# Storing x1 straight into the result, with the expert tiles scatter-adding there

## What is computed

```python
x = x + gnn(layernorm(x))            # relational graph convolution over 21,250 edges, 8 relations,
                                     # then tanh(u) * z + xn * (1 - z), z = [u, xn] @ w_gate + b_gate
# experts, on n = layernorm(x):
scores = softmax(n @ gate_w.T)       # 8 experts
top_scores, sel = top_k(scores, 2)   # each token goes to its 2 best
# tokens sorted by expert; for each expert e:
y = (silu(t @ w1[e]) * (t @ w3[e])) @ w2[e]       # 1024 -> 256 -> 1024
out = zeros.at[token].add(y * score)
x = x + out
```

## Time and profile before

| | |
|---|---|
| median of 3 runs | 1827.71 us |
| the profiled execution's own time | 1829.91 us |
| its span, first to last instruction | 1828.2 us |
| mean granted TensorE clock | 0.973 of full speed |
| PE busy / PEld busy | 1707.0 us (93%) / 1399.1 us (77%) |
| DVE / ACT / POOL busy | 1095.8 (60%) / 726.4 (40%) / 756.2 us (41%) |
| HBM traffic | 241.19 MB read, 102.15 MB written, 188 GB/s |

### The profile page before, as it was taken

How to read it: one execution, slowest core, us unless ns; L and a number is a source line. 1 busy time by engine, 2 the same in 40 slices (tenths; PEclk the granted TensorE clock), 3 DMA queues, 4 the chain that set the end, 5 groups by cost and what they waited for, 6 DMA issues and landing times. The chain is left out here.

```text
span 1828.2 us, 22117 instructions
## 1 busy us (share of the span) xinstructions
PE 1707.0 (93%) x7873; PEld 1399.1 (77%) x7873; DVE 1095.8 (60%) x1444; ACT 726.4 (40%) x1230; POOL 756.2 (41%) x663
## 2 busy tenths in 40 slices
PE   7999999999999999999998999989789958999993
PEld 6888888888888888888776777767678846878882
DVE  8555656665464342424599898899789876333200
ACT  2316656631231312121365565555522103454551
POOL 1001222226775656302355554545265515455531
PEclk9999999999999999999999999999899968999997
DMA  5236555466224343434788888888744436877645
GB/s 204 93 117 229 167 177 181 156 195 198 93 87 161 110 150 122 143 130 146 296 262 293 256 289 267 266 286 265 261 176 167 153 117 219 231 183 211 135 89 151
DMA packets 141050, 339.69 MB, mean 186 GB/s; under 512 B 19332, under 2 KB 35764, under 8 KB 140864
## 3 DMA queue, kind: packets, MB, share of 16 engines
q0 software_dynamic: 50816, 159.29, 29.2%
q1 hardware_dynamic: 90128, 179.00, 29.0%
HBM read 241.19 MB, written 102.15 MB: 188 GB/s over the span
## 5 line engine op out<-in xcount | busy, mean ns | idle before, releaser
L1056 POOL DMA_INDIRECT gathered<-Y,edge_row x184 | 220.5, 1198 | 218.2 <-PE banks L1215 189.4
L625 ACT ACTIVATE ghi<-gathered,edge_w 128x1024 fp32r<-128x1024 f32 x184 | 211.5, 1151 | 170.8 <-DMA gathered<-Y,edge_row 156.9
L945 DVE SCALAR_TENSOR_TENSOR glo<-gathered,edge_w,ghi 128x1024 fp32r<-128x1024 f32 x184 | 232.6, 1281 | 52.8 <-ACT ghi L625 51.1
L1032 POOL DMA_INDIRECT edge_w<-INV,edge_key x184 | 208.4, 1133 | 116.5 <-DMA edge_w<-INV,edge_key 84.9
L1073 PE MATMUL banks<-whi,xhi 128*128 128x512 f32 x640 | 252.7, 395 | 0.6 <-DVE xlo L768 0.6
L1075 PE MATMUL banks<-whi,xlo 128*128 128x512 f32 x640 | 249.8, 390 | 0.0
L1074 PE MATMUL banks<-wlo,xhi 128*128 128x512 f32 x640 | 249.7, 390 | 0.0
L1214 PE MATMUL banks<-ghi,sel 128*128 128x512 f32 x368 | 149.0, 405 | 25.6 <-DVE glo L945 24.3
L575 ACT ACTIVATE ring_hi<-raw_chunk 128x512 fp32r<-128x512 f32 x112 | 66.5, 624 | 207.5 <-PE banks L1177 127.6
L1215 PE MATMUL banks<-glo,sel 128*128 128x512 f32 x368 | 144.4, 392 | 0.0
L1073 PEld LDWEIGHTS banks<-whi,xhi 128*128 128x128 f32 x640 | 120.7, 189 | 25.5 <-DVE xlo L768 1.2
(11 more groups left out here) (316 smaller groups left out, 3670.9 us busy)
## 6 DMA issues: line engine op xcount, KB each, us to landing
raw<-in_L_ffn_w SPq DMA_DIRECT2D x24, 1024.0 KB
Y<-y_out SPq DMA_DIRECT2D x80, 256.0 KB
t_set<-in_L_gnn_weight POOLq DMA_DIRECT2D x64, 256.0 KB
TW<-t_set POOLq DMA_DIRECT2D x64, 256.0 KB
raw_chunk<-TW SPq DMA_DIRECT2D x64, 256.0 KB
w_stage<-in_L_gnn_weight SPq DMA_DIRECT2D x30, 512.0 KB, 5.0
raw_chunk<-in_L_gnn_weight SPq DMA_DIRECT2D x48, 256.0 KB
Y<-half_v SPq DMA_DIRECT2D x40, 256.0 KB
```

The source lines that it names most:

```text
L625: nc.scalar.activation(ghi[:, t % HR], gath[t % GR][:], ACT.Copy, scale=edge_w[:, t:t + 1]).then_inc(g_hi, 1)
L945: v.scalar_tensor_tensor(glo[t % GR][:], gath[t % GR][:], edge_w[:, t:t + 1], ghi[:, t % HR].bitcast(F32), ALU.mult, ALU.subtract).then_in ...
L1032: nc.gpsimd.indirect_dma_start(out=edge_w[:, t:t + 1], out_offset=None, in_=INV, in_offset=bass.IndirectOffsetOnAxis(ap=edge_key[:, t:t + ...
L1056: nc.gpsimd.indirect_dma_start(out=gath[t % GR][:], out_offset=None, in_=Y, in_offset=bass.IndirectOffsetOnAxis(ap=edge_row[:, t:t + 1], a ...
```

## The change

X1 is gone. In the gate stage x1 is stored straight into the result, of the last tile only its 98 rows, and the store for the dummy rows is gone. The scatter-adds go to the result, and the five copies at the end are gone with their wait. So the padded lanes need other rows, since the result has no dummy ones. A padded lane p of expert e now adds its zeros to row p, unless the token p is itself in the last tile of expert e; then it takes a row of 0 to 127 whose token is not there (some_row). No lane of a tile then adds zeros to a row to which another lane of the same tile adds its output. For this VectorE computes last_at (the position at which the last tile of each expert begins), in_last and spare (for the first 128 tokens) before it waits for the token lists. Then TensorE transposes spare (one small transpose), VectorE takes a maximum over it and spreads it, TensorE brings it to all lanes (one product with 8 rows), and VectorE picks for each tile its expert's entry (pad_row, 128x28x8) and puts it into add_i. The semaphore rt_poh now also counts these two hand-overs, and rt_placed (formerly rt_tok) the two answers. They lie in PSUM bank 6, in columns beside the logits; so TensorE waits for score_ready before its first output product into that bank (`outputs`).

```diff
--- before.py
+++ after.py
@@ -118,8 +118,6 @@
         YX = dram("YX", (2, NP, D))
         INV = dram("INV", (KEYS, 1))
         XN2 = dram("XN2", (NP, D))
-
-        X1 = dram("X1", (NP + P, D))
 
         def rows(j):
             return LASTP if j == NT - 1 else P
@@ -1310,15 +1308,13 @@
                         continue
                     d = j - 1
                     sp.wait_ge(x1_done, d + 1)
-                    sp.dma_start(X1[d * P:(d + 1) * P, :], x1[:, d % 2]).then_inc(x1_out[d % 2], 16)
-                    if d == 0:
-                        sp.dma_start(X1[NP:NP + P, :], x1[:, 0]).then_inc(x1_out[0], 16)
+                    sp.dma_start(out[d * P:d * P + rows(d), :], x1[:rows(d), d % 2]).then_inc(x1_out[d % 2], 16)
                     if d + 2 < NT:
                         fetch_x(d + 2)
                     sp.wait_ge(xn2_done, d + 1)
                     sp.dma_start(XN2[d * P:(d + 1) * P, :], xn2[:, d % 2]).then_inc(xn2_out[d % 2], 16)
                 for i in range(2):
-                    sp.wait_ge(x1_out[i], 16 * (NT // 2 + (i == 0)))
+                    sp.wait_ge(x1_out[i], 16 * NT // 2)
                     sp.wait_ge(xn2_out[i], 16 * NT // 2)
 
             @block.gpsimd
@@ -1418,7 +1414,7 @@
                     step(v.tensor_tensor(th[:, i], th[:, i], zg[:, i], ALU.mult))
                     dve.wait_ge(sum_done, j + 1)
                     if j >= 2:
-                        dve.wait_ge(x1_out[i], 16 * (j // 2 + (i == 0)))
+                        dve.wait_ge(x1_out[i], 16 * (j // 2))
                         dve.wait_ge(xn2_out[i], 16 * (j // 2))
                         dve.wait_ge(tx_done, 2 * (j - 1))
                     v.tensor_tensor(x1[:, i], xr[:, i], th[:, i], ALU.add).then_inc(x1_done, 1)
@@ -1554,14 +1550,19 @@
         sc = z5.put("sc", [P, 2, NT, 2], F32R)
         score = z5.put("score", [P, 2, MTE], F32)
         lane_row = z5.put("lane_row", [P, 1], F32)
+        last_at = z5.put("last_at", [P, X], F32)
+        in_last = z5.put("in_last", [P, X, 2], F32)
+        spare = z5.put("spare", [P, 3, X], F32)
+        some_row = z5.put("some_row", [P, P + 1], F32)
+        pad_row = z5.put("pad_row", [P, MTE, X], F32)
         add_s = z5.put("add_s", [P, 2, MTE], F32)
         add_i = z5.put("add_i", [P, MTE], I32)
         te = z5.put("te", [P, 2, MTE], F32)
         tile_expert = z5.put("tile_expert", [P, MTE], I32)
         first_tile = z5.put("first_tile", [P, X], I32)
-        rt_lg, rt_exp, rt_oh, rt_tot, rt_rank, rt_poh, rt_tok, rt_idx, rt_ready = (
+        rt_lg, rt_exp, rt_oh, rt_tot, rt_rank, rt_poh, rt_placed, rt_idx, rt_ready = (
             sem("shifted_logits_ready"), sem("exp_done"), sem("expert_onehot_ready"), sem("expert_totals_done"),
-            sem("expert_ranks_done"), sem("token_onehots_ready"), sem("tokens_placed"), sem("token_index_ready"),
+            sem("expert_ranks_done"), sem("token_onehots_then_spare_rows_ready"), sem("tokens_then_pad_rows_placed"), sem("token_index_ready"),
             sem("tile_expert_ready"))
         rt_iota = sem("token_numbers_ready")
 
@@ -1602,7 +1603,7 @@
         ye_done, ye_evac = sem("ye_done"), [sem(f"ye_evacuated{i}") for i in range(2)]
         ye_out = [sem(f"ye_stored{i}") for i in range(2)]
         assert HC == 2 and 2 * H == BANK
-        score_ready, out_stored = sem("scores_placed"), sem("out_stored")
+        score_ready = sem("scores_placed")
 
         with nc.Block() as block:
             @block.sync
@@ -1619,10 +1620,6 @@
 
                 sp.wait_ge(ye_out[0], 16 * ((MT + 1) // 2))
                 sp.wait_ge(ye_out[1], 16 * (MT // 2))
-                for j in range(0, NT, 2):
-                    at = slice(j * P, min(N, (j + 2) * P))
-                    sp.dma_start(out[at, :], X1[at, :]).then_inc(out_stored, 16)
-                sp.wait_ge(out_stored, 16 * (NT // 2))
 
             @block.gpsimd
             def _(pool):
@@ -1655,7 +1652,7 @@
                     if i >= 1:
                         pool.wait_ge(ye_out[(i - 1) % 2], 16 * ((i - 1) // 2 + 1))
                     nc.gpsimd.indirect_dma_start(
-                        out=X1, out_offset=bass.IndirectOffsetOnAxis(ap=add_i[:, i:i + 1], axis=0),
+                        out=out, out_offset=bass.IndirectOffsetOnAxis(ap=add_i[:, i:i + 1], axis=0),
                         in_=ye[:, i % 2], in_offset=None, compute_op=ALU.add).then_inc(ye_out[i % 2], 16)
 
                 for i in range(GX):
@@ -1816,15 +1813,34 @@
                 for c in range(C2):
                     v.tensor_scalar(poh_lo[:, c], iota[:, 0:P], p_lo[:, c:c + 1], None,
                                     ALU.is_equal).then_inc(rt_poh, 1)
-                dve.wait_ge(rt_tok, 1)
+                step(v.tensor_scalar(last_at[:], ce[:, 2, :], -float(P), None, ALU.add))
+                step(v.tensor_tensor(in_last[:], wit[:, :, 0:2], last_at[:].unsqueeze(2).to_broadcast([P, X, 2]),
+                                     ALU.is_ge))
+                step(v.tensor_tensor(in_last[:], in_last[:], oh_e[:, :, 0:2], ALU.mult))
+                step(v.tensor_reduce(spare[:, 0, :], in_last[:], AX.X, ALU.add))
+                step(v.tensor_scalar(lane_row[:], lanes[:], 1.0, None, ALU.add))
+                v.tensor_scalar(spare[:, 1, :], spare[:, 0, :], 0.5, lane_row[:], ALU.is_lt,
+                                ALU.mult).then_inc(rt_poh, 1)
+                dve.wait_ge(rt_placed, 1)
 
                 step(v.tensor_scalar(tok_s[:], psum[7][:, 0:MTE], -1.0, 0.0, ALU.add, ALU.max))
                 v.tensor_copy(tok_i[:], tok_s[:]).then_inc(rt_idx, 1)
 
                 step(v.tensor_copy(score[:, 1], psum[7][:, 2 * MTE:3 * MTE]))
-                step(v.tensor_scalar(lane_row[:], lanes[:], float(NP + 1), None, ALU.add))
+                dve.wait_ge(rt_placed, 2)
+                step(v.tensor_reduce(some_row[0:X, P:P + 1], psum[6][0:X, P:2 * P], AX.X, ALU.max))
+                v.tensor_copy(some_row[0:X, 0:P], some_row[0:X, P:P + 1].to_broadcast([X, P])).then_inc(rt_poh, 1)
                 step(v.tensor_tensor(score[:, 0], psum[7][:, MTE:2 * MTE], score[:, 1], ALU.add))
-                step(v.tensor_scalar(add_s[:, 0], psum[7][:, 0:MTE], 0.5, lane_row[:], ALU.is_lt, ALU.mult))
+                step(v.tensor_tensor(pad_row[:], te[:, 1, :].unsqueeze(2).to_broadcast([P, MTE, X]),
+                                     iota[:, 0:X].unsqueeze(1).to_broadcast([P, MTE, X]), ALU.is_equal))
+                dve.wait_ge(rt_placed, 3)
+                step(v.scalar_tensor_tensor(spare[:, 2, :], spare[:, 1, :], 0.5, psum[6][:, 2 * P:2 * P + X],
+                                            ALU.is_lt, ALU.mult))
+                step(v.tensor_tensor(spare[:, 2, :], spare[:, 2, :], spare[:, 1, :], ALU.add))
+                step(v.tensor_tensor(pad_row[:], pad_row[:], spare[:, 2, :].unsqueeze(1).to_broadcast([P, MTE, X]),
+                                     ALU.mult))
+                step(v.tensor_reduce(add_s[:, 1], pad_row[:], AX.X, ALU.add))
+                step(v.scalar_tensor_tensor(add_s[:, 0], psum[7][:, 0:MTE], 0.5, add_s[:, 1], ALU.is_lt, ALU.mult))
                 step(v.scalar_tensor_tensor(add_s[:, 1], psum[7][:, 0:MTE], -1.0, add_s[:, 0], ALU.add, ALU.add))
                 v.tensor_copy(add_i[:], add_s[:, 1]).then_inc(score_ready, 1)
 
@@ -1860,7 +1876,12 @@
                     pe.wait_ge(rt_poh, c + 1)
                     ins = pe.matmul(psum[7][:, 0:3 * MTE], poh_lo[:, c], place_val[:, c].rearrange("p a t -> p (a t)"),
                                     start=(c == 0), stop=(c == C2 - 1))
-                ins.then_inc(rt_tok, 1)
+                ins.then_inc(rt_placed, 1)
+                pe.wait_ge(rt_poh, C2 + 1)
+                pe.transpose(psum[6][0:X, P:2 * P], spare[:, 1, :], ident[:]).then_inc(rt_placed, 1)
+                pe.wait_ge(rt_poh, C2 + 2)
+                pe.matmul(psum[6][:, 2 * P:2 * P + X], some_row[0:X, 0:P], ident[0:X, 0:X],
+                          start=True, stop=True).then_inc(rt_placed, 1)
 
                 def expert_of(i):
                     return pe.value_load(tile_expert[0:1, i:i + 1], min_val=0, max_val=X - 1)
@@ -1925,6 +1946,8 @@
                     for c in range(2):
                         if i >= 1:
                             pe.wait_ge(ye_evac[c], i)
+                        elif c == 1:
+                            pe.wait_ge(score_ready, 1)
                         cols = slice(c * BANK, (c + 1) * BANK)
                         for k in range(HC):
                             at = slice(k * P, (k + 1) * P)
```

## The result

The changed kernel takes 1814.03 us, the median of 6 runs (1809.93 to 1816.36), the kernel before beside it 1827.8 (1825.35 to 1832.08). The ratio is 0.9916, 95% interval 0.9902 to 0.9929: 13 to 18 us less. Forecast were 1810.7 us and a range of 1808.6 to 1813.4; 0.9916 of the 1827.71 from which it was made is 1812.4. So the ratio lies inside the range, the median as measured 0.6 us above it. The profiled execution has a span of 1811.8 us against 1828.2, 16.4 us less (forecast: 1811.2).

A forecast was written before the change was run, and what follows sets the result against it. Five uncovered copies were taken to bound the end, a TensorE pipeline of 27 tiles the expert stage before. -18.0 - 0.7 + 0.4 + 1.3 = -17.0 us, taking the median from 1827.71 to 1810.7 us; range 1808.6 to 1813.4.

The forecast's parts named there:

- three signs: Wrong if scatters land over 10 us after issue, clock rises over 4.5 us after first transpose, tile 1's act_g stays 1.6.
- Step 1: Kernel's end: five copies of X1 into the result and their wait leave the path, -18.0 us; closing 0.47 us stays.
- Step 2: Gate stage: one 512 KB store fewer ahead of tile 2's xr fetch removes VectorE's wait, -0.7 us.
- Step 3: Routing: six small VectorE operations ahead of the token index, partly covered by idle time, delay the first gather, +0.4 us.
- Step 4's delay: Routing: remaining pad-row work, with the earlier additions, starts everything behind on VectorE 2.7 us later (2.1 to 4.0).
- Step 4's collision: Expert tile 1: expert 1's later load makes VectorE's splits and GpSimd's products block each other, TensorE idling, +1.3 us.
- Rival 3: Expert stage's start: TensorE's clock rises later, another 4.2 us stretch at half clock, +2.1, 1812.8 us; chance 0.11.
- Rival 1: Expert tile 1: no new collision, or tile 2's idle time goes in exchange; 1809.4 to 1808.4 us; chance 0.19.
- Rival 2: VectorE's additions and trips to TensorE cost more, the gate stage's gain lost; 1812.2 to 1812.9 us; chance 0.12.
- rival 4: Expert stage: scatter-adds into the result land slower and become the bound; 1831.5 us or more; chance 0.02.
- Rival 5: Last scatter or another transfer closes late, or x1 stores hold up buffers; some 3 us, 1814; chance 0.06.

The follow-up runs named there:

- e8: The changed kernel measured again, nothing altered; 1810.65 us, ratio 0.990 against the kernel before.
- e3: The kernel before without its five copies at the end and their wait, the result not written; span 1808.7 us.
- e1: The changed kernel plus a waited-for transfer of one row (4 KB) behind SyncE's wait for the last scatter-adds; span 1814.9 us.
- e2: The changed kernel plus a waited-for transfer of 256 rows (1 MB) behind SyncE's wait for the last scatter-adds; span 1813.5 us.
- e5: The changed kernel, GpSimd waiting for its last scatter-add to land before it leaves the block; span 1816.2 us.
- e4: The changed kernel with the 512 KB store of x1's first tile put back in SyncE's queue, into a scratch tensor; span 1819.6 us.
- e7: The changed kernel without the choice of pad rows, a padded lane p always adding its zeros to row p; span 1810.7 us.
- e9: The changed kernel with the choice of pad rows moved behind expert 0's splits, its TensorE steps behind the first products; 1812.72 us, ratio 0.9906 against the kernel before.
- e6: The changed kernel with expert 1's load issued only after w2 of expert 0 is split; span 1805.0 us.

## Why the prediction came out as it did

The sum was -17.0; the trace gave -16.4, the ratio -15.4 and that of e8 -18.3. The whole fits, but part of the fit is luck. The copies gave 1.85 us less than forecast; 0.7 of this came back because A, R and G were each a little better than their terms, and 0.5 from an earlier start and a shorter B, which the change doesn't touch. Two of the three signs by which the prediction would call itself wrong did come: the clock rose 6.2 us after the first transpose (over 4.5), and tile 1's act_g stayed at 1.59 us. The third did not: scatters landed 7.7 us after their issue (median), as before.

- **Step 1 (-18.0, bounds 17.5 to 18.5): a term mis-sized.** The copies are gone whole, as said, but "the closing 0.47 us stays" failed: it became 2.3, and T fell by 16.15 (15.95 in e3, where only the copies go). I had costed the removed cover as if nothing stood under it. e1 and e2 show that something did: some 2.3 us after the last scatter-add lands, which ran beside the copies; by e5 they are on GpSimd's side. The bound of 17.5 was drawn for just this and was too tight.
- **Step 2 (-0.7): right.** -0.83 in the profile, -1.0 between the means; the store put back brings the wait back (e4). The bound "not more than the wait" held for that execution only, as the wait itself ranges to 1.54.
- **Step 3 (+0.4): mis-sized by half.** +0.18. The count and the cover (0.87) were right; six small operations took 1.15 us from the first's start to tok_s, not 1.26, and the last one-hot's row lies over the first of them by another tenth.
- **Step 4's delay (2.7 us, 2.1 to 4.0): right.** 2.35 us. Nothing that I called covered showed up: "minus", expert 0's weights, the scores, and the wait in the first output.
- **Step 4's collision (+1.3): the mechanism exists, the forecast change in it did not come.** Forecast were an act_g above 2 us in tile 1 and TensorE idle 1 to 2 us for it; it took 1.59 as before, and TensorE idled 0.23. I had the load of expert 1 move by the full 2.7 us. It moved against the first gather by 1.1 us (19.06 to 20.15), since the gathers were out of its way and it flew 9.8 us instead of 11.0. Tile 1 lost 0.34 us, between prod_s's ask and act_g's end (2.44 to 2.78). The rest of A's +0.91 is the first gather's landing (+0.21) and TensorE's slow start, next point. e3 has the kernel before's code there, and still act_g takes 2.65 in tile 1: how hard the two collide is drawn anew in each execution. A is 36.4, 38.7, 38.0 and 38.0 without the choice ahead of the splits (before, e3, e7, e9), and 37.2 to 40.9, mean 39.1, with it (after, e1, e2, e4, e5, e8). The means lie 1.3 us apart, but most of this isn't the collision: e1 and e2 hold a second fall of the clock (1.6 to 1.7 us each), and e4 and e5 had the longest first stretch at half clock (next point). The collision's own part, from prod_s's ask to act_g's end in tile 1, is 2.78 to 4.25 us, mean 3.6, with the choice ahead and 2.44 to 3.87, mean 3.1, without. These ranges overlap; whether the choice as such costs more in A than the 0.34 us of this one profile stays open.
- **Rival 3 (the clock rises later, +2.1) happened, at a lower price.** The windows view of the changed kernel:

```profile
1514.60:1520.60 6.00, 5.96 (x19) 4.20 (x20) 5.93 (x5) 3.56 (x6) 0.91 (x1) 0.50 0.61 227
```

TensorE ran at half clock (0.50) for 6.2 us from its first transpose instead of 4.3. Its third group of transposes came 11.79 us after the first, against 11.48: 0.3 us, while an idle gap of 0.55 us ahead of the first products went in exchange. In e4 and e5 half clock lasted about 9 us, in e8 4.4, and the first transpose lay 14.3 and 14.4 us ahead of prod_s of tile 0 against 12.6. So the rival's price, 2.1, is near what a late rise can cost (1.8); this profile paid 0.3. The moment of the rise differs between executions of equal code, and with it the phase in which tile 1's products meet the splits. That the clock can fall again once the experts' products run (e6 above) was in no term and no rival.
- **Rivals 1, 2, 4 and 5.** Rival 1 (no new collision) is nearest to what tile 1 did; its 1809.4 needed the 18.0 of step 1. Rival 2's operations did not cost more (steps 3 and 4 above). The scatter-adds kept their pace: 6.68 us between the last two, B unchanged, and they land 7.7 us after issue (median) as before, so rival 4's mechanism didn't show. Rival 5 named a late close among its cases, at 3 us; 1.8 came.

## What to carry to other kernels

Before counting a removed tail as gained, ask what else ends the block: the other engines' way out, here 2.3 us after the last scatter's landing, runs under a transfer and comes to light when it goes. Where VectorE and GpSimd both work in a pipeline, start VectorE's long operations after GpSimd's short product that the pipeline waits for, not at the event that also triggers it: two added waits gave 7 us by the medians and 10 by the stretch concerned, about half of what the change gave. And if single executions differ by more than the effect, cut the traces into stretches between events of the same code; some of them agree to 0.3 us. Look at the granted clock in each stretch before comparing it: a fall to half clock cost as much here as the effect sought.

## What the runs showed of the hardware

A transfer of 2.0 us issued by SyncE after the last scatter-add landed was free, and GpSimd's waiting for its own last scatter cost 3.0 us (11.4 against 8.4 us from issue to end): here, leaving the block with the scatter-add in flight was cheaper than waiting for it first. A load of 2 MB issued in nearly the same surroundings landed after 9.8, 11.0 and 14 us. And an operation's row can begin long before it works: act_g's 2.65 us in e6 are 0.6 after VectorE's subtraction has ended and 2 of standing behind it. TensorE's granted clock rose 3.9 to 9.2 us after the first transposes in nearly equal code (in the changed kernel's trace TensorE was busy for 5.96 of the 6.00 us at half clock that the windows row shows), and in four of thirteen traces it fell to half once more, within 2 us after TensorE had idled 1.6 to 1.7 us; each fall cost 1.6 to 1.7 us.
